# Decoder layer on one core: self attention unrolled by batch, with row-tiled scores, a table as mask and sums from a column of ones

## The reference

```python
q, k, val = (proj(Wq), proj(Wk), proj(Wv))
R_hat = (1.0 + jnp.exp(vv)) / (1.0 + jnp.exp(vv - wv * R))      # R = |i - j|
scores = jax.nn.relu(jnp.einsum('bhqd,bhkd->bhqk', q, k)) * R_hat[None]
scores = jnp.where(causal[None, None], -jnp.inf, scores)
attn = jax.nn.softmax(scores / np.sqrt(hd), axis=-1)
ctx = jnp.einsum('bhqk,bhkd->bhqd', attn, val) ... ; return ctx @ Wo + bo
x = _layernorm(x + self_attention(x)); x = _layernorm(x + cross_attention(x, ctx_1024)); x = _layernorm(x + ffn(x))
```

## Time and profile before

| | us |
|---|---|
| median of 3 runs (2991.63 to 2994.65) | 2994.35 |
| the profiled execution | 2993.32 |
| its span, first to last instruction | 2991.5 |
| stage B, first scores (240.6) to last result (489.5) | 248.9 |
| stage C, first to last instruction (493.35 to 680.9) | 187.5 |
| PE / PEld busy, of the span | 2852.2 / 2325.2 |
| DVE / ACT / POOL busy, of the span | 1625.1 / 1370.1 / 697.6 |

### The profile page before, as it was taken

How to read it: one execution, slowest core, us unless ns; L and a number is a source line. 1 busy time by engine, 2 the same in 40 slices (tenths; PEclk the granted TensorE clock), 3 DMA queues, 4 the chain that set the end, 5 groups by cost and what they waited for, 6 DMA issues and landing times. The chain is left out here.

```text
span 2991.5 us, 61181 instructions
## 1 busy us (share of the span) xinstructions
PE 2852.2 (95%) x23108; PEld 2325.2 (78%) x23108; DVE 1625.1 (54%) x3198; ACT 1370.1 (46%) x3837; POOL 697.6 (23%) x662
## 2 busy tenths in 40 slices
PE   7997997898999999999999999999999958999998
PEld 7994554787878788877888788887878738889987
DVE  5116996773555555555655555555555542443342
ACT  2116995212555555555555555555555544223221
POOL 1114443332121121211212112121121002333332
PEclk9999998999999999999999999999999969999999
DMA  4326442752121111211102111121111032110000
GB/s 149 127 110 154 110 110 89 250 191 84 30 58 29 45 42 30 58 30 45 42 30 58 30 45 42 30 58 30 45 42 30 12 114 91 54 46 32 28 32 18
DMA packets 144010, 197.76 MB, mean 66 GB/s; under 512 B 58576, under 2 KB 83152, under 8 KB 143768
## 3 DMA queue, kind: packets, MB, share of 16 engines
q1 hardware_dynamic: 143768, 194.40, 20.9%
HBM read 141.30 MB, written 53.07 MB: 65 GB/s over the span
## 5 line engine op out<-in xcount | busy, mean ns | idle before, releaser
L1216 DVE TENSOR_REDUCE D_neg_max<-D_ps_s 100x1 f32<-100x722 f32 x512 | 441.5, 903 | 541.8 <-PE D_ps_s L1284 540.9
L1170 ACT ACTIVATE D_pT<-D_ps_t 128x300 f32<-128x300 f32 x1024 | 375.8, 419 | 352.7 <-PE D_ps_t L1296 321.7
L1178 ACT ACTIVATE D_e<-D_ps_s,D_neg_max 100x722 f32<-100x722 f32 x512 | 438.6, 872 | 1.9 <-DVE D_neg_max L1216 1.9
L1149 POOL CAST D_ctx_high<-D_craw 128x722 fp32r<-128x722 f32 x124 | 104.6, 844 | 1277.3 <-PE D_ps_p L64 1244.0
L1296 PEld LDWEIGHTS D_ps_t<-D_ident,D_e 100*128 100x128 f32 x3072 | 302.7, 142 | 100.5 <-issue 89.9
L1296 PE MATMUL D_ps_t<-D_ident,D_e 100*128 100x100 f32 x3072 | 367.0, 256 | 3.6 <-ACT D_pT L1170 3.2
L64 PE MATMUL D_ps_p<-D_ctx_high,cross_wk_high 128*128 128x362 f32 x1024 | 358.4, 350 | 11.5 <-DVE D_ctx_low L1237 11.5
L1224 DVE TENSOR_SCALAR D_e<-D_e,D_inv 100x722 f32<-100x722 f32 x512 | 334.4, 653 | 18.1
L64 PE MATMUL D_ps_p<-D_ctx_high,cross_wk_low 128*128 128x362 f32 x1024 | 337.2, 329 | 0.0
L64 PE MATMUL D_ps_p<-D_ctx_low,cross_wk_high 128*128 128x362 f32 x1024 | 336.6, 329 | 0.0
L1161 ACT ACTIVATE D_values<-D_ps_p 128x512 f32<-128x512 f32 x192 | 114.5, 596 | 465.1 <-PE D_ps_p L64 465.1
(11 more groups left out here) (182 smaller groups left out, 5473.2 us busy)
## 6 DMA issues: line engine op xcount, KB each, us to landing
D_craw<-in_ctxT SPq DMA_DIRECT2D x126, 361.0 KB, 3.5
D_queries<-cross_q SPq DMA_DIRECT2D x64, 200.0 KB, 3.8
A_xraw<-in_xT SPq DMA_DIRECT2D x5, 1280.0 KB, 8.6
self_q<-A_q SPq DMA_DIRECT2D x5, 1280.0 KB, 4.7
self_k<-A_k SPq DMA_DIRECT2D x5, 1280.0 KB, 5.5
self_v<-A_v SPq DMA_DIRECT2D x5, 1280.0 KB, 5.9
B_q<-self_q SPq DMA_DIRECT2D x16, 400.0 KB, 3.4
B_kdiag<-self_k SPq DMA_DIRECT2D x64, 100.0 KB, 3.3
```

Of the source, the lines that this page charges most:

```text
L1149: pool.tensor_copy(cs[b % 2][0][:, k, :], craw[k % 2][:, :]).then_inc(c_high, 1)
L1170: act.activation(pT[quad % 2][:, 3 * half:3 * half + 3, h % 4 * T:(h % 4 + 1) * T], ps_t[half][:, 0:3 * T].rearrange("p (a t) -> p a t", a=3),
L1178: act.activation(e[n % 4][:, 0:S].rearrange("p (a b) -> p a b", a=2), both_banks(n), ACT.Exp, bias=neg_max[:, n % 4:n % 4 + 1], accum_out= ...
L1216: dve.tensor_reduce(neg_max[:, n % 4:n % 4 + 1], both_banks(n), AX.XY, ALU.max, negate=True)\
```

## The change

Stage A stores the values as `v_d` [3200, 16 x 33]: behind the 32 columns of each head stands one column of ones, set once by POOL. The table's fill above the diagonal is -2^100 instead of -1, and there is no mask product. Stage B is unrolled by batch, and each engine's unit is a batch (16 heads) where it can be:

- PE: the scores are 16 products (m, j) of 32 rows each, `tile_position=(32 j, 0)`, 100 moving columns, into four PSUM banks, one per j. The transposes are the same 16 per batch. For the values the probabilities are the loaded operand (100 columns) and `v` the moving one (33 columns), 16 products per batch; the 33rd column is the sum.
- DVE: one relu, floor and table product over 100 x 1600, one maximum over it, and twice per batch a reciprocal of 8 sums out of PSUM and a product of 100 x 256.
- POOL: one addition of the negated maxima over 100 x 1600.
- ACT: two exponentials of 100 x 800 without bias or sum, and four copies of transposed tiles of 100 x 400.
- SP: q and k in one transfer each, the table in four, one store of [100, 512] per batch; `self_o` is [3200, 512].

Stage C is unrolled, transposes `self_o` on PE (20 more transposes of 128 x 128 a group) and splits it out of PSUM (ACT and DVE), gives two PSUM banks to that and leaves two for `project_q`, and loads x ahead of the store of x1.

The core of the diff (loads, stores and the engines' loops of both stages cut):

```diff
-MASK = 1.5 * 2.0 ** 127
+MASK = 2.0 ** 100
+FLOOR = 2.0 ** -90
+HV = HD + 1
@@ phase_qkv
+                        for v in vo:
+                            pool.memset(v[:, :, :, HD:HV], 1.0).then_inc(consts, 1)
@@ phase_self_attention
+                for b in range(B):
+                    pool.wait_ge(max_done, b + 1)
+                    heads = s_rel[b % 2][:, :, :].rearrange("p j (m t) -> p (j m) t", t=T)
+                    pool.tensor_tensor(heads, heads, neg_max[:, b % 2, :].unsqueeze(2).broadcast_to([T, H, T]), ALU.add)\
+                        .then_inc(sub_done, 1)
@@ scalar
+                for s in range(B + 2):
+                    if s >= 2:
+                        take_transposed(s - 2, 0)
+                        take_transposed(s - 2, 1)
+                    if 1 <= s <= B:
+                        exps(s - 1, 0)
+                    if s >= 2:
+                        take_transposed(s - 2, 2)
+                        take_transposed(s - 2, 3)
+                    if 1 <= s <= B:
+                        exps(s - 1, 1)
@@ vector
+                for s in range(B + 3):
+                    if s >= 3:
+                        take_result(s - 3, 1)
+                    if s < B:
+                        scale_max(s)
+                    if 2 <= s < B + 2:
+                        take_result(s - 2, 0)
...
+                def scores(b):
+                    wait(pe, rel_done, b)
+                    for m in range(QUADS):
+                        for j in range(4):
+                            r = slice(HD * j, HD * (j + 1))
+                            last = pe.matmul(ps_s[0:T, j, m * T:(m + 1) * T], qs[p % 2][r, m, t:t + T],
+                                             ks[p % 2][r, m, t:t + T], start=True, stop=True, tile_position=(HD * j, 0))
...
+                def transposes(b, m):
+                    if m == 0:
+                        pe.wait_ge(exp_done, 2 * (b + 1))
+                    wait(pe, pT_done, QUADS * b + m - 1)
...
+                def weighted_sum(b, m):
+                    for j in range(4):
+                        c, h = (4 * (m % 2) + j) * HV, (4 * m + j) * HV
+                        last = pe.matmul(ps_o[m // 2][0:T, c:c + HV], pT[m % 2][:, j, :], vs[p % 2][:, b % 2, h:h + HV],
+                                         start=True, stop=True)
@@ tensor
+                for s in range(B + 3):
+                    if 2 <= s < B + 2:
+                        transposes(s - 2, 0)
+                    if s >= 3:
+                        weighted_sum(s - 3, 3)
+                    if 2 <= s < B + 2:
+                        transposes(s - 2, 1)
+                    if s < B:
+                        scores(s)
+                    if 2 <= s < B + 2:
+                        weighted_sum(s - 2, 0)
+                        transposes(s - 2, 2)
+                        weighted_sum(s - 2, 1)
+                        transposes(s - 2, 3)
+                        weighted_sum(s - 2, 2)
@@ phase_norm_and_queries
+    TURN_AFTER = {0: 0, 2: 1, 3: 2, 5: 3, 6: 4}
+                def transpose_o(g, i):
+                    for k in range(KD):
+                        last = pe.transpose(ps_ot[n % 2][:, k * P:(k + 1) * P], orow[:, i, k * P:(k + 1) * P], ident[:, :])
...
+                        if u in TURN_AFTER and g + 2 < NG:
+                            transpose_o(g + 2, TURN_AFTER[u])
```

More of the change, by code:

```diff
@@ L424, in phase_self_attention @@
         s_done, rel_done, max_done = sem("B_s_done"), sem("B_rel_done"), sem("B_max_done")
[L425 to L446, removed]
+        sub_done, exp_done = sem("B_sub_done"), sem("B_exp_done")
+        t_done, pT_done, pv_done = sem("B_t_done"), sem("B_pT_done"), sem("B_pv_done")
+        inv_done, o_done = sem("B_inv_done"), sem("B_o_done")
+        stored = [sem("B_stored0"), sem("B_stored1")]
         with nc.Block() as block:
@@ L470, in load_v @@
[L470 to L486, removed]
+                def load_qk(p):
+                    wait(sp, s_done, 2 * p - 2)
+                    for rows, dst in ((q_rows, qs), (k_rows, ks)):
+                        sp.dma_start(dst[p % 2][:, :, :], rows[:, :, col(p * 2 * T, 2 * T)]).then_inc(qk_loaded[p % 2], 16)
@@ L487, in _ @@
+                load_qk(0)
+                for j in range(4):
+                    sp.dma_start(rhat[:, j, :, :], rhat_d.rearrange("t (m j s) -> t j m s", j=4, m=QUADS)[:, j, :, :])\
+                      .then_inc(rhat_loaded, 16)
+                load_v(0)
+                load_qk(1)
+                load_v(1)
                 for raw, dst in zip(next_w, staging):
                     sp.dma_start(dst[:, :, :], raw.rearrange("(k p) n -> p k n", p=P)).then_inc(w_loaded, 16)
[L489 to L496, removed]
@@ L497, in _ @@
-                for p in (PAIRS - 2, PAIRS - 1):
-                    store(p, p % 2)
+                for p in range(PAIRS):
+                    if p + 2 < PAIRS:
+                        load_qk(p + 2)
+                    for b in (2 * p, 2 * p + 1):
+                        store(b)
+                    if p + 2 < PAIRS:
+                        load_v(p + 2)
                 for par in range(2):
-                    sp.wait_ge(stored[par], 64 * (PAIRS // 2))
+                    sp.wait_ge(stored[par], 16 * (B // 2))
@@ L524, in step @@
-                def step(p, par, n, s):
-                    if started(n, 2):
-                        normalise(n - 2, s - 2)
-                quads(pool, step)
-                for back in (2, 1):
-                    normalise(QUADS * B - back, STEPS - back)
-            LAG = 5
+                for b in range(B):
[3 more added lines that the diff above has]
+                        .then_inc(sub_done, 1)
@@ L559, in _, with exps, take_transposed @@
-                quads(act, step)
-                for back in range(LAG, 0, -1):
-                    take_result(PAIRS - 1, QUADS * B - back, STEPS - back)
+                def exps(b, half):
+                    act.wait_ge(sub_done, b + 1)
+                    wait(act, t_done, QUADS * (b - 1))
+                    two = slice(2 * half, 2 * half + 2)
+                    act.activation(e[b % 2][:, two, :], s_rel[b % 2][:, two, :], ACT.Exp).then_inc(exp_done, 1)
+                def take_transposed(b, m):
+                    quad = QUADS * b + m
+                    act.wait_ge(t_done, quad + 1)
+                    wait(act, pv_done, quad - 1)
+                    act.activation(pT[m % 2][:, :, :], ps_t[m % 2][0:T, 0:QT].rearrange("p (j t) -> p j t", j=4),
+                                   ACT.Copy).then_inc(pT_done, 1)
```

448 lines of the change are left out of this document (172 added, 276 removed).

## The result

| | before | after |
|---|---|---|
| median of 4 runs, us | 2994.46 (2991.63 to 2994.65) | 3067.39 (3066.07 to 3071.07) |
| ratio, 95% interval | | 1.0248 [1.023, 1.0266] |
| profiled span | 2991.5 | 3064.8 |
| mean granted clock | 0.977 | 0.929 |
| first scaling of B (the table product) | 244.5 | 240.1 |

The change makes the kernel 2.5% slower. The last two rows locate it: B's last result comes 71.6 us later, the stretch from there to D's first product (stage C) grows by another 6.6 us (202.3 to 208.8), and D and E, which are not touched, give 4.9 back. (This is one profiled execution of each.

What follows compares the result with a forecast made beforehand. Stage B was taken as bound by ACT, with PE and DVE just behind. Span 2991.5, plus 82 for B and 2 for C, gives 3075.5; with 1.8 outside the span, 3077 us. Own range 3045 to 3110; 8 in 10, 2950 to 3110.

Steps and rivals of the forecast that it cites:

- likeliest case: Stage B loses the full clock and PE at 1.2 GHz sets a 10.0 us step: 3077 us, chance 0.55.
- The clock: Stage B: the new step, 2.9 us of columns in 6.4, is too thin, so the granted clock is 0.50.
- PE at 1.2 GHz: Stage B, per batch: transposes 2.67, scores 1.65, values 5.35, wait 0.3, together 10.0 us, with PE the bound.
- ACT, DVE, POOL: Stage B, per batch: ACT 3.8, DVE 4.9, POOL 3.5 us; none can hold a step longer than 5 us.
- The full clock, first rival: Stage B keeps 2.4 GHz: 6.4 us a step, B 38 us shorter, 2957 us; chance 0.22.
- The chain: Stage B at full clock: a two-step loop through PE, DVE, POOL and ACT, 12.8 us, 6.4 a step.
- the wait that it named: Stage B at full clock: POOL's addition, 3.5 us, stands on the two-step loop of 12.8 us while PE idles.
- In series, third rival: Stage B at 1.2 GHz: load and product one after the other, 13 us a step, 3175 us; chance 0.04.
- B's end: Stage B: scores of batch 0 worth 241, then 33 steps of 10.0, ending at 571 us, +82.
- Stage C: More transposes on PE, partly beside waits, against earlier x loads: +2 us, between -8 and +10.
- D and E: The stages after C: no term in the forecast's sum, so no change.

Runs made afterwards that it cites:

- 3 and 1: Changed kernel plus unread PE products before B and in its first two steps, then three at each step's head, one before third transposes: 2961.09 us, ratio 0.9886.
- 1 and 0: Changed kernel plus unread PE products before B and in its first two steps, then one at each step's head: 3064.53 us, ratio 1.0231.
- halves with 2 and 0: Changed kernel plus unread start products and two at each step's head, with the maximum and POOL's addition in two halves each: 2947.13 us, ratio 0.9842.

## Why the prediction was right

Its likeliest case happened, through the mechanism that it named, 10 us above the measurement. By parts of the profiled spans: B 10.4 us less than forecast, C 4.6 more, D and E 4.9 less; the last two nearly cancel by chance.

- **The clock.** Forecast 0.50 over B, found 0.50 from 231.1 to 579.3. Its reasoning, that the step is too thin for the clock, is borne out by the run with extra products at the start only. Its list of what else the step holds, "weight loads, handovers and gaps", was not told apart: gaps of 0.43 to 0.60 us a step did not lose the clock beside seven extra products, and with no gap at all it did not come back. That nothing in B would bring it back held through 290 us of a fully occupied PE.
- **PE at 1.2 GHz.** Transposes 2.67, found 2.88; scores 1.65, found 1.60; values 5.35, found 5.13; wait 0.3, found 0.26. Sum 10.0 and 9.87. The errors cancel in part. That values cost a full load per pass, taken from the transposes, was the term with the widest bounds (2.7 to 7.1) and the best one to have settled: the 8 passes of a group take 1.24 to 1.36, 0.155 to 0.17 each.
- **ACT, DVE, POOL.** ACT 2 x 0.862 + 4 x 0.504 = 3.74, forecast 3.8. DVE 1.83 + 1.82 + 2 x (0.20 + 0.42) = 4.9, forecast 4.9. POOL was the one mis-sized, 2.86 for 3.5: narrow and very wide instructions of other kinds did not give its slope. It cost nothing at 1.2 GHz.
- **The full clock, first rival.** Forecast 6.4 a step and 2957 us. With the clock held: scores 0.89 (forecast 0.87), steps 6.01, 2948 us. The chain was 0.3 to 0.4 long by POOL's size, and the loop through the second exponential was not seen. Counterfactual though it was, it came near what the change is worth with the clock held, but not by the wait that it named: making the maximum and the addition of that chain in halves did not move the step.
- **In series, third rival.** Refuted. A load's record is 0.286 and a product's 0.347, on the same rows, and they start every 0.155 to 0.17: the next load runs while the product is in flight. The Trainium skill (TensorE: Matmul & The Clock Gate, Part 3: Packing small matmuls) says in its list of what overlaps that this is so only between different row groups; the measurement decides against that line. The same section of the Trainium skill (Part 3: Packing small matmuls) also lets a load into a background weight buffer run ahead, and with that the rows agree.
- **B's end.** 571, found 561: the first scores start at 236.8, 4.2 earlier than the 241 of the sum; the first two steps, which have few or no transposes and values, take 5.14 + 7.96 us and not 20; 29 x 0.13 less in the others. Against that, 25.0 us pass from the last scores to the last result where the sum had two steps, 20.
- **Stage C.** +2, found +6.6 (+3.3 to +9.5 by the eleven other profiles), inside the bounds. The sum charged the transposes but no wait at its head. The rows of after on PE:

```profile
570.82 1.94 PE L860 MATMUL C_ps_ot<-C_ident,C_orow 128*128 128x128 f32 x8 [10.42 <-DMA C_orow<-self_o]
573.32 1.97 PE L860 MATMUL C_ps_ot<-C_ident,C_orow 128*128 128x128 f32 x8 [0.56 <-DVE C_o_low L770]
576.62 0.78 PE L66 MATMUL C_ps_y<-self_wo_high,C_o_high 128*128 128x512 f32 x1
```

The first wide product comes 15.5 us after B's last result, before it came after 12.3: the transposes need a whole group's load and take turns with DVE, at 1.2 GHz. That is 3.2 of the 6.6; the other 3.4 lie in the groups after it, were not taken apart, and are no more than what this stretch differs by from profile to profile.
- **D and E** came out 4.9 us shorter, forecast zero. Among the thirteen other profiles this stretch is 2291 to 2299 us, before's was 2300. No run tests it, and I leave it open.

## What to carry to other kernels

Before a stage is thinned on TensorE, ask whether it keeps the granted clock: with the clock held the change was worth 1.6% here, without it it lost 2.5%. Price the new step at both levels, and measure the version with a few unread products beside it, started before the stage. That is a probe and not a guarantee: two or more a step held the clock in all 22 executions with POOL's addition made once, by their mean clocks of 0.976 to 0.982, but seven a step in only 6 of 8 with it made twice, and one a step in neither of two. Turning a product round so that the wide operand is loaded and the narrow one streamed made each pass cost a load here: 0.155 to 0.17 us at 1.2 GHz for 100 columns loaded and 33 streamed.

## What was not expected of the hardware

- A PE that was occupied throughout did not regain the clock. With two extra products a step and no start, PE's records cover 290.0 of 290 us and the loads' 277.8, at 0.50 throughout. The Trainium skill (TensorE: Matmul & The Clock Gate, Part 1: The HAM clock gate) says the full clock comes after PE has been kept busy; read by the records' busy time, this trace disagrees. In the head of C the clock came back in every profile, 13 to 18 us after B's last result. In four of them (the value products as before, 3 and 1, 1 and 0, halves with 2 and 0) it was back before the first wide product, when PE had done nothing since B but transposes of 128 x 128.
- The same step both keeps 2.4 GHz (steps of 6.01) and stays at 1.2 GHz (10.49), depending on where it started. And a gap of 0.43 to 0.60 us in each step goes with 1.00 in one run (seven extra products), none with 0.50 in another (two).
- At 1.2 GHz a group of four transposes takes 0.67 to 0.70 us beside value products of the same tile, and 0.83 beside tiles of 64 columns or ahead of 32-row tiles: changing the tile shape costs some 0.15.
